# Reciprocals of the softmax denominators spread over rows by a broadcast transfer through device memory instead of TensorE, and pair loads ahead of the weight words

## What is computed

```python
qh = softmax(Wq @ layernorm(x), over the 64 rows of a head) * 64 ** -0.5   # 8 heads
kh = softmax(Wk @ ctx, over the 512 columns)
context = kh @ vh.T                                                        # 64 x 64 per head
out = Wo @ (context.T @ qh) + bo
x = x + tanh(g_xattn) * out / norm(out over channels) * g * 8
x = x + tanh(g_ffn) * down(silu(gate(layernorm(x))) * up(layernorm(x)))    # 4-bit weights, 512 -> 1376 -> 512
```

## Time and profile before

| what | us |
|---|---|
| median of 3 runs (lowest, highest) | 816.8 (812.04, 819.32) |
| the profiled execution's own time | 815.45 |
| its span | 813.7 |
| TensorE busy in the span | 731.1 (90%) |
| VectorE busy | 612.2 (75%) |
| ScalarE busy | 436.6 (54%) |
| 14 steps, from the den_sq issue of step 1 to that of step 15 | 396.32 |

### The profile page before, as it was taken

How to read it: one execution, slowest core, us unless ns; L and a number is a source line. 1 busy time by engine, 2 the same in 40 slices (tenths; PEclk the granted TensorE clock), 3 DMA queues, 4 the chain that set the end, 5 groups by cost and what they waited for, 6 DMA issues and landing times. The chain is left out here.

```text
span 813.7 us, 13752 instructions
## 1 busy us (share of the span) xinstructions
PE 731.1 (90%) x4551; PEld 392.8 (48%) x4551; DVE 612.2 (75%) x806; ACT 436.6 (54%) x764; POOL 186.2 (23%) x317
## 2 busy tenths in 40 slices
PE   4889988988998999999999966399999999999997
PEld 3544553554454455455545532135555555555555
DVE  6377776877878777787778554399988877877885
ACT  3766665665666667566665632144443445334443
POOL 5122222213213222321322211211121112211121
PEclk9999999999999999999999996599999999999999
DMA  3021312321330321122020000100000000100001
GB/s 99 9 76 32 81 23 67 81 50 37 80 82 5 82 67 26 48 67 69 11 63 18 5 6 1 63 10 1 1 1 27 27 0 13 39 0 0 26 26 52
DMA packets 29195, 29.89 MB, mean 37 GB/s; under 512 B 18628, under 2 KB 18756, under 8 KB 29036
## 3 DMA queue, kind: packets, MB, share of 16 engines
q1 hardware_dynamic: 26972, 28.85, 13.1%
q10 hardware_dynamic: 2192, 0.66, 0.3%
HBM read 23.49 MB, written 4.23 MB: 34 GB/s over the span
## 5 line engine op out<-in xcount | busy, mean ns | idle before, releaser
L1300 DVE SCALAR_TENSOR_TENSOR acc<-ffn_bank,scale_T,acc 128x512 f32<-128x512 f32 (+1 forms) x264 | 186.7, 748 | 39.6 <-PE ffn_bank L1253 34.1
L1252 PE MATMUL ffn_bank<-ek,w_gu 128*128 (+3 forms) x352 | 137.9, 392 | 2.8 <-PEq L90 1.8
L1253 PE MATMUL ffn_bank<-ekT,w_gu 128*128 (+3 forms) x352 | 134.4, 382 | 0.0
L1160 POOL TENSOR_TENSOR in_lo<-inter,in_hi 128x512 fp32r<-128x512 f32 (+1 forms) x44 | 56.4, 1282 | 229.9 <-ACT in_hi L1199 229.9
L1192 ACT ACTIVATE act_gate<-acc 128x512 f32<-128x512 f32 (+1 forms) x44 | 27.7, 630 | 144.3 <-DVE acc L1300 144.3
L985 DVE TENSOR_TENSOR eq<-eq,pair 128x1024 f32<-128x1024 f32 x64 | 78.0, 1220 | 25.1 <-PE pair L741 25.1
L493 ACT ACTIVATE eq<-pair 128x1024 f32<-128x1024 f32 x64 | 65.6, 1025 | 55.0 <-PE pair L761 55.0
L977 DVE TENSOR_REDUCE qmax<-pair 128x16 f32<-128x1024 f32 x64 | 77.6, 1212 | 14.9 <-PE pair L623 14.6
L484 ACT ACTIVATE ek<-pair,kneg 128x512 f32<-128x512 f32 x128 | 86.6, 685 | 3.6 <-DVE kneg L980 3.5
L1269 PE MATMUL ffn_bank<-wd_hi,in_hi 128*128 128x512 f32 (+1 forms) x176 | 86.7, 531 | 0.4 <-DVE wd_lo L1333 0.4
L1269 PE MATMUL ffn_bank<-wd_lo,in_hi 128*128 128x512 f32 (+1 forms) x176 | 86.7, 531 | 0.0
(11 more groups left out here) (138 smaller groups left out, 1168.7 us busy)
## 6 DMA issues: line engine op xcount, KB each, us to landing
xall<-in_x SPq DMA_DIRECT2D x16, 256.0 KB, 3.9
ctx_raw<-in_ctx SPq DMA_DIRECT2D x16, 256.0 KB, 4.1
out_x<-xall SPq DMA_DIRECT2D x16, 256.0 KB, 2.0
zero<-zeros_plus SPq DMA_DIRECT2D x8, 344.0 KB, 4.0
packed<-in_L_ffn_gate_qweight SPq DMA_DIRECT2D x4, 688.0 KB
packed<-in_L_ffn_up_qweight SPq DMA_DIRECT2D x4, 688.0 KB
packed<-in_L_ffn_down_qweight SPq DMA_DIRECT2D x10, 256.0 KB
d_scale<-in_L_ffn_down_scales SPq DMA_DIRECT2D x1, 1408.0 KB, 6.1
```

What stands on the lines that cost most here:

```text
L1252: pe.matmul(gu_bank[job % 4][0:w, :], lhsT, xT_hi[:, g, rows], start=True, stop=False)
L1253: pe.matmul(gu_bank[job % 4][0:w, :], lhsT, xT_lo[:, g, rows], start=False, stop=True).then_inc(gu_mm, 1)
L1300: dve.scalar_tensor_tensor(out=acc[0:w, it % 3, m, :], in0=gu_bank[job % 4][0:w, :], scalar=scale_T[0:w, it, 4 * m + g:4 * m + g + 1], in1 ...
```

## The change

- **Spread.** `spread_reciprocals`, the matrix `spread`, `rden_parts` and `rden_rows` are gone, with the two split operations of VectorE. The reciprocals (128 x 64) are written to a tensor in device memory, `rden_all` (32 KB, one transfer). SP waits until that has landed, and then issues four transfers that each read 8 KB of it with a partition broadcast into 64 partitions of `rden_spread` (2 batches x 8 KB per partition): 4 x 64 x 8 KB = 2 MB (2.097 million bytes) per step. `normalise(t)` multiplies by `rden_spread` in SBUF, and `normalise(0)` alone waits for all four transfers.
- **Order on TensorE.** `t_logits(0)` no longer waits for the last `normalise`, and `ctx_transposed` moves from the step's end to behind `k_transposed(0)` (on ACT its copy moves likewise).
- **Order on VectorE.** `reciprocals` comes behind `maxima(1)` instead of `maxima(2)`, and `ss_max` behind `normalise(0)` instead of before the unpacking.
- **Order on SP.** The pair p+2 is loaded before the weight words.
- **Smaller ones.** ACT rounds the next pair's context (`ctx_high`) at the step's start, GpSimd does `ctx_low` before the layernorm's moments, the rows of `head_sum` are permuted so that the heads come out in the order that the transfers need, and the scratch space for GpSimd's transfers is set to 2048.

```diff
                     sp.wait_ge(rden_ready, r + 1)
+                    sp.dma_start(rden_all.rearrange("b s e n -> (b s e n)").rearrange("(p m) -> p m", m=C),
+                                 rden[:, :]).then_inc(rden_out, 16)
+                    sp.wait_ge(rden_out, 16 * (r + 1))
                     for b in range(2):
-                        for part in range(2):
-                            rows = b * C + part * HEADS
-                            sp.dma_start(rden_rows[rows:rows + HEADS, :].bitcast(F32).rearrange("r (k m) -> r k m", m=C),
-                                         rden_parts[half(b), part, :].bitcast(F32)).then_inc(rden_gathered, 16)
+                        for e in range(2):
+                            sp.dma_start(rden_spread[half(e), b, :, :].rearrange("p (s t) n -> p s (t n)", s=2),
+                                         rden_all[b, :, e, :].partition_broadcast(C)).then_inc(rden_in, 16)
...
-                if following:
-                    load_weights(p + 1, *following)
                 if project and more:
                     sp.wait_ge(ct_mm, p + 1)
                     load(p + 2, par)
+                if following:
+                    load_weights(p + 1, *following)
...
                     if t == 0:
                         pe.wait_ge(x_hi, p + 1)
-                        if residual:
-                            pe.wait_ge(q_norm, 4 * r)
-                        elif combine:
+                        if combine:
                             pe.wait_ge(t_max, 4 * p)
...
                 def normalise(t):
-                    dve.wait_ge(b_mm, 4 * r + t + 1)
+                    if t == 0:
+                        dve.wait_ge(rden_in, 64 * (r + 1))
                     e = eq[:, 1 - par, t, :, :]
-                    dve.tensor_tensor(e, e, dve_pair[:, :, :], ALU.mult).then_inc(q_norm, 1)
+                    dve.tensor_tensor(e, e, rden_spread[:, :, t, :], ALU.mult).then_inc(q_norm, 1)
...
                 def reciprocals():
                     dve.wait_ge(den_spread, 64 * (r + 1))
-                    dve.reciprocal(rden[:, :], den_sq[:, :]).then_inc(rden_step, 1)
-                    dve.wait_ge(rden_step, 2 * r + 1)
                     if residual:
-                        dve.wait_ge(rden_gathered, 64 * r)
-                    dve.tensor_copy(rden_parts[:, 0, :], rden[:, :]).then_inc(rden_step, 1)
-                    dve.wait_ge(rden_step, 2 * r + 2)
-                    dve.tensor_tensor(rden_parts[:, 1, :], rden[:, :], rden_parts[:, 0, :].bitcast(F32),
-                                      ALU.subtract).then_inc(rden_ready, 1)
+                        dve.wait_ge(rden_out, 16 * r)
+                    dve.reciprocal(rden[:, :], den_sq[:, :]).then_inc(rden_ready, 1)
...
-                if residual:
-                    dve.wait_ge(ss_spread, 32 * (r2 + 1))
-                    dve.tensor_scalar(ss_max[:, :], ss_sq[:, :], 1e-24, None, ALU.max).then_inc(ss_bounded, 1)
                 if weights:
                     nibbles(p, *weights)
                 if combine:
                     normalise(0)
+                if residual:
+                    dve.wait_ge(ss_spread, 32 * (r2 + 1))
+                    dve.tensor_scalar(ss_max[:, :], ss_sq[:, :], 1e-24, None, ALU.max).then_inc(ss_bounded, 1)
```

More of the change, by code:

```diff
@@ L41 @@
 POOL_CONSTS = 25
-DVE_CONSTS = 6
+DVE_CONSTS = 5
 DOWNS = 4
@@ L403, in _ @@
                 for tt in range(2):
-                    then(pool.memset(head_sum[half(e), tt, :].rearrange("o (m f) -> o m f", f=4)[:, :, 2 * tt + e],
+                    then(pool.memset(head_sum[half(e), tt, :].rearrange("o (m f) -> o m f", f=4)[:, :, 2 * e + tt],
                                      float(DH) ** 0.5))
@@ L535, in step @@
                     return
+                if not last:
+                    ctx_high(p + 1, i + par, 1 - par)
                 if combine:
@@ L539, in step @@
                 k_exp_tile(0, 1)
-                if not last:
-                    ctx_high(p + 1, i + par, 1 - par)
                 if residual:
@@ L727, in fold_context @@
                     last.then_inc(m_mm, 1)
-                def spread_reciprocals(t):
-                    if not combine:
-                        return
-                    if t == 0:
-                        pe.wait_ge(rden_gathered, 64 * (r + 1))
-                        if project:
-                            pe.wait_ge(t_max, 4 * p + 4)
-                        else:
-                            pe.wait_ge(q_norm, 4 * r)
-                    else:
-                        pe.wait_ge(q_norm, 4 * r + t)
-                    for b in range(2):
-                        last = pe.matmul(dve_pair[:, b, :], spread[half(b), t, :], rden_rows[half(b), :],
-                                         start=True, stop=True)
-                    last.then_inc(b_mm, 1)
                 def q_logits(t):
@@ L878, in step @@
                 spread_inverse_norm()
-                spread_reciprocals(3)
                 q_logits(3)
                 k_transposed(3)
-                ctx_transposed()
             step(0, 0, 0, True, False, False)
@@ L1002, in step @@
                     maxima(1)
+                    if combine:
+                        reciprocals()
                     if not last:
```

46 lines of the change are left out of this document (20 added, 26 removed).

## The result

The changed kernel takes 909.2 us (median of 4 runs, 908.13 to 911.91) where the kernel before takes 815.5 in the same comparison; the ratio is 1.115 (95% interval 1.109 to 1.121). The profiled execution has a span of 906.3 us and an own time of 908.13, 92.7 above that of before. The prediction was 884 (798 to 915) and slower: the sign and the mechanism came out as forecast, the time is 25 us longer.

The account below looks back on a forecast made before the run. TensorE was taken to set the period of 28.3 us, and a 33.2 us closed loop through the broadcast after the change. 64 us for 13 intervals, 2 for the first, 3 for the drain: 815.45 + 69 = 884 us (798 to 915).

Parts of the forecast that it names:

- Item 1: In the loop, the first multiplication, normalise(0), on VectorE after the broadcast lands: 1.21 us.
- Item 2: In the loop, ss_max and the inverse norm on GpSimd until SP issues rn_rows, previously hidden: 3.13 us.
- Item 3: In the loop, the two small transfers of rn_rows, from issue to reader's start: 2.35 us.
- Items 4 and 5: TensorE's spread_inverse_norm, q_logits(3) and k_transposed(3), 0.41 and 2.04 us; then next step's work until den_sq's issue, 3.73 us.
- The clock term: TensorE's clock falls each step after its stand, halving speed for the first 3.5 us of Items 4 and 5: 1.75 us more.
- Item 6: In the loop, the den_sq transfers: 2.83 us to issue four and 1.2 to land, 4.0 us.
- Items 7 and 8: The reciprocal and its hand-over, 0.54 and 0.1 us; then the write to device memory, 2.0 us.
- Items 9 and 10: The broadcast from device memory: its fixed part, 2.7 us, then its 2.097 MB of data, 9.2 us.
- 13 x (33.2 - 28.3): Loss over 13 step intervals, predicted loop of 33.2 us against 28.3 now: 64 us.
- The cost at nothing: Copies moved on ACT, ctx_transposed and GpSimd's order only shift work inside idle time: nothing, 0.6 us at most.
- the clock that stays up: Rival: same loop with TensorE's clock not falling, 31.4 us per step, 861 us in all; chance 0.24.
- the fast broadcast: Rival: broadcast data at d_scale's 428 GB/s, loop 27.1 us, 799 us in all, deciding from 344 GB/s; chance 0.15.

Follow-up runs that it names:

- e2: The changed kernel with only batch 0's two broadcasts, both batches multiplied by them, so half the bytes: 819.2 us, ratio 1.006 to the kernel before.
- e5: The changed kernel with 24 pairs of unread matmuls ahead of TensorE's wait for rn_rows: 890.4 us, ratio 1.090 to the kernel before.
- e6: The changed kernel with spread_inverse_norm moved behind the next step's k_logits(0): 873.7 us, ratio 1.071 to the kernel before.
- e3: The changed kernel with each broadcast taking the previous step's reciprocals, issued right behind den_sq: 856.5 us, ratio 1.052 to the kernel before.
- e9: The kernel before with the early pair load and the changed kernel's two orders on VectorE: 806.8 us, ratio 0.987 to the kernel before.
- e12: e9 with ctx_transposed behind k_transposed(0) and ScalarE's copy of its result moved with it: 782.2 us, ratio 0.961 to the kernel before.
- e10: The changed kernel with ss_max ahead of the first multiplication again: 901.7 us, ratio 1.107 to the kernel before.
- e11: The changed kernel with ss_max and the context folding ahead of the first multiplication, ss_sq and rn_rows issued by ScalarE's queue: 953.5 us, ratio 1.170.
- e1: The changed kernel with two 1 MB broadcasts to 128 partitions instead of four of 512 KB to 64: 853.5 us, ratio 1.047 to the kernel before.
- e8: The whole change without the broadcast, TensorE still spreading the reciprocals: 787.1 us, ratio 0.966 to the kernel before.

## Why the prediction was right, and where it was short

The time lies in the range, and the mechanism was the one forecast: a closed loop through the broadcast, longer than TensorE's own work, in which everything saved on TensorE and VectorE disappears. e2 (half the bytes, 819), e5 (clock, 890), e6 (TensorE's order, 874) and e3 (latency ahead of the broadcast, 856) each shortened it by one link. The signs named at the end of the prediction are there: VectorE's wait (7.8 to 9.1 us), TensorE's stand (6.9, "about 6"), the rate (207), the half clock, and the bn_stats wait gone. One was not: the period was to be 31 to 34 us and alike in both kinds of step, and it is 34.1 to 36.0 in gate/up steps and 34.0 to 34.2 in down steps. Item by item, in the step shown:

- Item 1, 1.21: 1.14, from one start to the next. The choice of the same time from SBUF as from PSUM was right (1.218 us, no gain).
- Item 2, 3.13: 3.91 (332.70 to 336.61). I had read GpSimd's two small operations at 0.20 us, their time before; they took 0.77 and 1.06.
- Item 3, 2.35: 2.62. Items 4 and 5 and the clock, 2.45 + 3.73 + 1.75 = 7.93: 4.19 + 3.75 = 7.94 (339.23 to 343.42 to 347.17). The clock term, the choice least supported by a row, was right here, and e5 bears it out with 1.63 in the mean.
- Item 6, 4.0: 4.21 to the reciprocal's start. Items 7 and 8, 0.64 + 2.0: 2.04 from there to the broadcast's issue; the 32 KB write took 1.45 and not the 2.0 of a 256 KB one.
- Items 9 and 10, 2.7 + 9.2 = 11.9: 12.26. 207 GB/s make 10.1 us for the data and leave 2.1 for the fixed part, so 9.2 was too fast and 2.7 too slow; the two misses nearly cancel.

The loop is 34.1 us here and 34.54 in the mean of 13 steps (68.83 to 517.87), where the prediction had 33.2. In that mean item 2 is 0.7 us over the forecast and items 9 and 10 are 0.6 over (12.52 us; in the step from 103.74 it is 13.63); items 3, 6, and 4 and 5 with the clock are 0.2 to 0.3 over each, and the write is 0.6 under. The step from 139.02, the longest with 35.99 us, has 12.97 for items 9 and 10 and 9.16 for items 4 and 5 with the clock; why these two differ from step to step, no run shows. Before, the same 13 steps took 28.52 in the mean (68.19 to 439.01), not 28.3, so that they lost 78.2 us where the sum had 64, 14 more. The first interval gave 0.4 us (25.92 against 25.50) where I took 2.

**What the sum left out** is a turn of the loop: "13 x (33.2 - 28.3)", with the drain at 3 us. It stops at step 15's den_sq, but step 15's own broadcast lies behind that issue, and the loop runs once more before the drain's den_sq: 11.1 us that no term held. A turn like the others accounts for 6.0 of them (34.54 against 28.52). The other 5.1 belong to this turn, which goes on into the output matmuls of the drain: TensorE had half clock for 10 us, and 16 of those matmuls took 5.38 us, where before they took 3.65 at the full one; and from the first multiplication to rn_rows went 6.3 us instead of 4.9, since one of GpSimd's small operations took 2.77.

```profile
545.00:550.00 5.00, 4.70 (x17) 3.01 (x17) 3.03 (x5) 1.07 (x2) 1.29 (x5) 0.50 0.01 3
550.00:555.00 5.00, 3.97 (x12) 1.22 (x14) 0.00 (x0) 0.98 (x1) 1.36 (x5) 0.55 0.02 3
...
551.03 5.38 PE L661 MATMUL small<-eq,fold 128*64 128x512 f32 x16 [1.11 <-ACT ekT L489]
```

The drain itself gave 3.2, the 3 that I took, between 0 and 10; since no run takes it apart, that is luck as far as is known. 14 - 2 + 11 = 23 is the difference between 884 and the profiled execution's 908.1, to 1 us.

**The cost at nothing** that should have been looked at is another: "only shift work inside time in which ACT and GpSimd are idle". ctx_transposed on TensorE does shift nothing of weight on its own engine, but it releases SP's loads, and so decides what lies ahead of den_sq. Without the broadcast that is worth 22 to 25 us (e9 806.8 and e12 782.2; by their ratios, 0.987 and 0.961, 22). In the changed kernel the reciprocal starts 4.1 to 4.4 us behind den_sq's issue in every step, so nothing of it is in the loop. The same holds for my reading of item 2 as a matter of VectorE's order alone: ss_sq was behind the broadcast in any case (e10, e11), which the prediction didn't ask of the queue.

Of the rivals, the clock that stays up is out: it fell behind the stands of 6.9 us (after), 4.0 (e1) and 3.5 (e3), and behind 7 of 13 stands of some 2 us (e2); the fast broadcast fell with 207 GB/s. Even e1's 303 are below the 344 from which it would have won.

What stays open: whether a broadcast that doesn't hold up the inverse norm could come near 782 us. e11 was meant to show it and did not, for the wait that it put on ScalarE.

## What to carry to other kernels

A result that goes through device memory and comes back as megabytes costs its latency (here 2.04 + 12.3 us from reciprocal to reader) in every turn of the loop that it closes; follow the loop from landing to landing before counting what the busiest engine saves, and count the turn that is under way when the loop ends. Small transfers that were waited for paid here for the large ones issued ahead of them, on the same queue or on another engine's (e9, e10, e11): ask of each moved instruction whose transfers it releases. Take such a change apart: here a loss of 94 us hid parts worth 32.

## What the runs showed of the hardware that was not expected

- GpSimd's operations of 128x8, 0.20 us before, take 0.77 and 1.06 us (2.77 once, at 539.53 us) beside VectorE operations with two inputs in SBUF; in the timeline above L352 ends with VectorE's L945 (334.67 + 0.77 = 335.44 against 335.38). With the multiplication reading PSUM (e8) they take 0.21 and 0.20. In one step there they run from 190.87 to 191.35 us, wholly beside such a multiplication (190.58 to 191.80). The operation of 2.77 us ends at 542.30, with the two multiplications that ran beside it (539.88 to 542.23). The Trainium skill, "SBUF — State Buffer", section "Who interferes with whom", says that a VectorE instruction with two SBUF inputs contends with a GpSimd instruction that reads SBUF, and calls their shared ports an exclusive lock; the trace agrees.
- A 2 KB transfer issued behind 2 MB lands with them, some 10 us later, from the same queue (10.3 us, e10) and from another engine's (9.7, e11).
- Broadcasts of the same 2 MB from device memory: 207 GB/s in four to 64 partitions, 303 in two to 128.
- TensorE's clock fell to half behind stands of 1.9 to 2.5 us in 7 steps of e2 and stayed at full behind stands of 2.0 to 2.7 us in the 6 others, at 1.5 us each time in the loop.
